# Feed-forward rows: down product one body later, two block-scale products moved from VectorE to GpSimd

## The reference, cut to what matters

```
x = x + mx_linear(silu(mx_linear(n, w_gate)) * mx_linear(n, w_up), w_down)     # n = layernorm(x)
mx_linear(a, w) = q_act(a) @ q_w(w).T
q_act(a): per block of 32 elements of a row:
    scale = 2 ** (floor(log2(max |a|)) - 2)
    q     = clip(round a / scale to 3 fraction bits, -7.5, 7.5) * scale
```

## Time and profile before

| | us |
|---|---|
| median of 3 runs | 880.72 (877.41 to 882.65) |
| the profiled execution, its own time | 882.03 |
| its span, first to last instruction | 880.0 |
| PE / DVE / POOL / ACT busy | 778.0 / 653.6 / 551.4 / 399.5 |
| mean granted PE clock | 0.957 |

### The profile page before, as it was taken

One profiled execution on the slowest core, in us unless ns is written; L12 is line 12 of the kernel. 1 busy time (PEld: TensorE's weight loads), 2 busy tenths in 40 slices (PEclk: granted clock), 3 DMA queues, 4 the chain that ended last, 5 costly groups with the idle time before them and its releaser, 6 DMA issues. The chain is left out here.

```text
span 880.0 us, 14839 instructions
## 1 busy us (share of the span) xinstructions
PE 778.0 (88%) x4808; PEld 543.6 (62%) x4808; DVE 653.6 (74%) x1162; ACT 399.5 (45%) x1074; POOL 551.4 (63%) x543
## 2 busy tenths in 40 slices
PE   3899999587999999689999999999999999756675
PEld 1545454255877777566777777777777777524443
DVE  4898998366788787656656777988697669489883
ACT  2678787442222232224554444554444444533443
POOL 3555555313666767636657778787878787445674
PEclk9899999886999999979999999999999999978999
DMA  9200000012000010042210000000000000000001
GB/s 257 87 2 0 0 0 1 1 64 95 19 19 19 18 38 33 0 144 66 69 47 1 1 1 2 1 1 1 1 1 1 1 1 1 1 0 13 18 31 37
DMA packets 8762, 24.12 MB, mean 27 GB/s; under 512 B 1711, under 2 KB 5167, under 8 KB 8087
## 3 DMA queue, kind: packets, MB, share of 16 engines
q1 hardware_dynamic: 8154, 23.28, 8.1%
q10 hardware_dynamic: 549, 0.08, 0.1%
HBM read 21.26 MB, written 2.10 MB: 27 GB/s over the span
## 5 line engine op out<-in xcount | busy, mean ns | idle before, releaser
L1457 POOL TENSOR_TENSOR q<-turned 64x512 f32<-64x512 f32 x128 | 168.2, 1314 | 28.9 <-DVE turned L1381 11.8
L1144 PE MATMUL ps<-l_yt,a 128*128 128x512 f32 x576 | 150.7, 408 | 0.3 <-DVE l_yt L1346 0.3
L1144 PEld LDWEIGHTS ps<-l_yt,a 128*128 128x128 f32 x576 | 104.8, 191 | 32.1 <-DVE turned L1381 7.3
L1278 ACT ACTIVATE p<-ps,l_negmax 128x128 f32<-128x128 f32 x256 | 91.3, 384 | 59.8 <-DVE l_negmax L1372 59.8
L1444 POOL TENSOR_TENSOR p<-p,l_inverse 128x512 f32<-128x512 f32 x64 | 67.1, 1048 | 80.1 <-DVE l_inverse L1403 79.9
L1381 DVE TENSOR_TENSOR turned<-ps,rope 128x1024 f32<-128x1024 f32 x64 | 78.0, 1219 | 37.3 <-PE ps L1144 26.3
L765 PE MATMUL ps<-yt_experts,wsplit 128*128 (+1 forms) x384 | 98.3, 406 | 4.7 <-DVE h L854 2.9
L394 DVE TENSOR_REDUCE negmax<-ps 128x4 f32<-128x512 f32 x128 | 85.3, 687 | 10.7 <-PE ps L243 8.9
L765 PEld LDWEIGHTS ps<-yt_experts,wsplit 128*128 128x128 f32 x384 | 71.3, 192 | 22.3 <-issue 4.1
L325 ACT ACTIVATE pt<-ps 128x512 f32<-128x512 f32 x128 | 72.8, 597 | 7.8 <-PE ps L263 3.8
L1393 DVE TENSOR_TENSOR turned<-ps,rope 64x512 f32<-64x512 f32 (+1 forms) x96 | 65.5, 683 | 2.4 <-PE ps L1144 1.0
(11 more groups left out here) (186 smaller groups left out, 1617.6 us busy)
## 6 DMA issues: line engine op xcount, KB each, us to landing
wide<-in_wide SPq DMA_DIRECT2D x8, 768.0 KB, 4.2
mx_raw<-in_mx SPq DMA_DIRECT2D x8, 384.0 KB, 3.1
x<-in_x SPq DMA_DIRECT2D x4, 512.0 KB, 9.3
ctx_t<-in_ctx_t SPq DMA_DIRECT2D x1, 2048.0 KB, 7.5
out<-x SPq DMA_DIRECT2D x16, 128.0 KB, 1.7
narrow<-in_narrow SPq DMA_DIRECT2D x8, 192.0 KB, 2.8
ktraw<-in_ctx_rows SPq DMA_DIRECT2D x1, 1248.0 KB
wraw<-in_gate SPq DMA_DIRECT2D x1, 1024.0 KB, 18.7
```

The source lines that it names most:

```text
L1144: out = pe.matmul(tile_ps[t % 2], a[i][:, pa, kin, k * 128:(k + 1) * 128], yt[j % 2][:, py, kin, :, :].rearrange("p b s -> p (b s)"), star ...
L1278: t = act.activation(p[:, head, s, :], s_ps[head][:, s * S:(s + 1) * S], ACT.Exp, bias=negmax[:, head, s:s + 1], accum_out=total[:, head, ...
L1457: t = pool.tensor_tensor(out[rows[(head + half) % 2], head, :], turned[rows[head], half, :], turned[rows[head], 2 + half, :], ALU.add)
```

## The change

- PE, ACT: the transposes of a batch, and their copy, move from body n-2 to n-3, the down product from n-3 to n-4, with the semaphore counts and buffer indices moved alike; `steps` has one body more (B + 7). The copy of the result stays at n-4. PE's order within a body (gate and up, down, transposes) stays.
- Last group of the front: `divide` and the product `multiply` go to POOL, ahead of its other work of bodies 5 and 7; the clip between them becomes a part of its own, `clip`, in DVE's body 5. The turn moves from PE's body 7 to 9.
- Groups 0 to 2 (latent attention): the same instructions stay on DVE in the same order; `divide` waits by itself for the scales and loses its `carry`, and the clip has one more wait.

```
-                for k, part in (..., (7, f.divide), (8, f.multiply)):
+                for k, part in (..., (7, f.divide), (8, f.clip), (8, f.multiply)):
...
-    def divide(self, dve, m, j):
-        wait(dve, self.yc_made, j)
-        carry(dve, m)
+    def divide(self, engine, m, j):
+        engine.wait_ge(self.y_step, SCALE_STEPS * (j + 1))
+        wait(engine, self.yc_made, j)
...
-    def multiply(self, dve, m, j):
+    def clip(self, dve, m, j):
         dve.wait_ge(self.y8_made, j + 1)
+        wait(dve, self.yq_made, j)
         carry(dve, m)
         dve.tensor_scalar(self.yc[:, :], self.y8[:, :], ...).then_inc(self.yc_made, 1)
-        dve.wait_ge(self.yc_made, j + 1)
-        wait(dve, self.yq_turned, j)
-        dve.tensor_tensor(self.blocks(self.yq), ...
+    def multiply(self, engine, m, j):
+        engine.wait_ge(self.yc_made, j + 1)
+        wait(engine, self.yq_turned, j)
+        engine.tensor_tensor(self.blocks(self.yq), ...
...
-        LAST, TURN_LAST = GROUPS - 1, 7
+        LAST, TURN_LAST = GROUPS - 1, 9
...
-            for n in range(B + 6):
+            for n in range(B + 7):
...                                                   # PE
-                if inside(n - 3, B):
+                if inside(n - 4, B):
-                    pe.wait_ge(hq_kept, n - 2)
-                    wait(pe, x_made, n - 4)
-                    pe.matmul(down_ps[old], m.ident[:, :], m.x[:, n - 3, :], start=True, stop=False)
+                    pe.wait_ge(hq_kept, n - 3)
+                    wait(pe, x_made, n - 5)
+                    pe.matmul(down_ps[par], m.ident[:, :], m.x[:, n - 4, :], start=True, stop=False)
...
-                if inside(n - 2, B):
-                    pe.wait_ge(hq_made, n - 1)
-                    wait(pe, hq_kept, n - 2)
+                if inside(n - 3, B):
+                    pe.wait_ge(hq_made, n - 2)
+                    wait(pe, hq_kept, n - 3)
...                                                   # ACT
-                if inside(n - 2, B):
-                    act.wait_ge(hq_turned, n - 1)
-                    wait(act, down_made, n - 3)
-                    act.activation(hqt[par][:, :], h_ps, ACT.Copy).then_inc(hq_kept, 1)
+                if inside(n - 3, B):
+                    act.wait_ge(hq_turned, n - 2)
+                    wait(act, down_made, n - 4)
+                    act.activation(hqt[old][:, :], h_ps, ACT.Copy).then_inc(hq_kept, 1)
...                                                   # DVE
-                for k, part in ((0, f.statistics), (2, f.normalise), (3, f.scales), (4, f.divide), (5, f.multiply)):
+                for k, part in ((0, f.statistics), (2, f.normalise), (3, f.scales), (5, f.clip)):
...                                                   # POOL
+                if n == 5:
+                    f.divide(pool, m, LAST)
+                if n == 7:
+                    f.multiply(pool, m, LAST)
```

More of the change, by code:

```diff
@@ L1433, in _ @@
                     normalise(n // PAIRS + 1)
-                for k, part in ((2, f.add), (3, f.statistics), (5, f.normalise), (6, f.scales), (7, f.divide), (8, f.multiply)):
+                for k, part in ((2, f.add), (3, f.statistics), (5, f.normalise), (6, f.scales), (7, f.divide), (8, f.clip), (8, f.multiply)):
                     if front_in(n, k) is not None:
@@ L1556, in scales @@
         block_scale(dve, then, self.yscale[:, :], self.yinverse[:, :], self.UNIT)
-    def divide(self, dve, m, j):
-        wait(dve, self.yc_made, j)
-        carry(dve, m)
-        dve.tensor_tensor(self.blocks(self.y8), self.blocks(self.y), spread(self.yinverse[:, :], 2, MX),
+    def divide(self, engine, m, j):
+        engine.wait_ge(self.y_step, SCALE_STEPS * (j + 1))
+        wait(engine, self.yc_made, j)
+        engine.tensor_tensor(self.blocks(self.y8), self.blocks(self.y), spread(self.yinverse[:, :], 2, MX),
                           ALU.mult, saturate=False).then_inc(self.y8_made, 1)
-    def multiply(self, dve, m, j):
+    def clip(self, dve, m, j):
         dve.wait_ge(self.y8_made, j + 1)
+        wait(dve, self.yq_made, j)
         carry(dve, m)
@@ L1568, in multiply @@
                           ALU.min, ALU.max).then_inc(self.yc_made, 1)
-        dve.wait_ge(self.yc_made, j + 1)
-        wait(dve, self.yq_turned, j)
-        dve.tensor_tensor(self.blocks(self.yq), self.blocks(self.yc), spread(self.yscale[:, :], 2, MX),
+    def multiply(self, engine, m, j):
+        engine.wait_ge(self.yc_made, j + 1)
+        wait(engine, self.yq_turned, j)
+        engine.tensor_tensor(self.blocks(self.yq), self.blocks(self.yc), spread(self.yscale[:, :], 2, MX),
                           ALU.mult).then_inc(self.yq_made, 1)
@@ L1658, in body @@
                             t.then_inc(made, 1)
-                if inside(n - 3, B):
-                    if n == 3:
+                if inside(n - 4, B):
+                    if n == 4:
                         pe.wait_ge(f.x_mid, GROUPS)
-                    pe.wait_ge(hq_kept, n - 2)
-                    wait(pe, x_made, n - 4)
-                    pe.matmul(down_ps[old], m.ident[:, :], m.x[:, n - 3, :], start=True, stop=False)
+                    pe.wait_ge(hq_kept, n - 3)
+                    wait(pe, x_made, n - 5)
+                    pe.matmul(down_ps[par], m.ident[:, :], m.x[:, n - 4, :], start=True, stop=False)
                     for k in range(FFN // 128):
-                        t = pe.matmul(down_ps[old], hqt[old][:, k * S:(k + 1) * S], m.wq[:, 2, k * E:(k + 1) * E],
+                        t = pe.matmul(down_ps[par], hqt[par][:, k * S:(k + 1) * S], m.wq[:, 2, k * E:(k + 1) * E],
                                       start=False, stop=(k == FFN // 128 - 1))
@@ L1676, in body @@
                     for k in range(FFN // 128):
-                        t = pe.transpose(h_ps[:, k * S:(k + 1) * S], hq[par][:, k * 128:(k + 1) * 128], m.ident16[:, :])
+                        t = pe.transpose(h_ps[:, k * S:(k + 1) * S], hq[old][:, k * 128:(k + 1) * 128], m.ident16[:, :])
                     t.then_inc(hq_turned, 1)
```

## The result

Eight executions each, taken side by side: 877.90 us before, 872.11 us after, by their medians. One of the eight after took 2499 us; the other seven lie between 870.11 and 875.04, their median is 870.77, and the ratio leaves the slow one out: 0.9919, 95% interval 0.9894 to 0.9945. So the change makes the kernel 0.8% faster, about 7.1 us (4.8 to 9.3). Forecast were 7.5 us less, and a time of 873.2 us (869.5 to 878.0). That time was reckoned from a median before of 880.72; from the 877.90 of this comparison, 7.5 less would be 870.4. The gain is therefore what to compare, not the time.

What follows compares the result with a forecast made beforehand. Steady feed-forward bodies alternate between DVE's own 4.64 us and 5.22, set by a round over POOL, PE and ACT. Gains of 1.82 + 1.72 + 3.12 and 0.84 in the drain, 7.5 us, gave 873.2 us (869.5 to 878.0).

Steps and rivals of the forecast that it cites:

- Divide off DVE: Feed-forward body 4: moving the last group's divide to POOL takes DVE's body from 6.46 to 4.64, gain 1.82 us.
- Clip and product: Body 5: product leaves DVE, clip stands behind one POOL product; 7.04 instead of 8.76 us, gain 1.72 (0 to 3.5).
- Shift: Transposes and down product one body later: each feed-forward body that waited falls to DVE's 4.64 us, gain 3.12.
- The round: Feed-forward loop over POOL, PE and ACT: 9.9 us carrying two bodies, 4.93 each; with three bodies, 3.3 each.
- The turn in body 9: PE's body 9: turn adds some 1.8 us before the next gate, which still ends by C(10) with 0.7 to spare.
- Drain: After the last combine: down product starts when the turned rows are there, about 0.4 us at two bodies; gain 0.84.
- PE at the lower clock: Rival: PE bodies beyond 4 and 5 at half clock lose 3.0 us each; with four, 885.2 us; chance 7%.
- Other engines within a hair: Rival: PE, ACT or POOL, within 0.8 us of DVE's pace, keep bodies near 4.9; 877.2 us; chance 14%.
- Earlier lock or full clock: Rival: clip gets the lock first (1.8 us) and the drain keeps full clock (1.7); 869.7 us; chance 12%.

Runs made afterwards that it cites:

- psum_clip: Changed kernel with the last group's clip as a scalar_tensor_tensor, lower limit read from PSUM; 66.25 us from combine 4 to last ACT copy, ratio to before 0.9867.
- shift_only: Changed kernel with the last group's divide and product back on DVE; 72.48 us from combine 4 to last ACT copy, ratio to before 0.9957.
- dve_probe: Changed kernel plus one small unused reciprocal on DVE in each body; 69.25 us from combine 4 to last ACT copy, against 68.70 for the changed kernel.
- pool_probe: Changed kernel plus one unused 128x256 product on POOL in each body; 68.73 us from combine 4 to last ACT copy, against 68.70 for the changed kernel.
- pool_only: Kernel before with the last group's divide and product on POOL, turn in PE's body 9; 76.10 us from combine 4 to last ACT copy, ratio 0.9978.

## Why the prediction was right

- *Divide off DVE:* forecast 1.82, measured 6.46 - 4.64 = 1.82; `hq` beside it back from 2.89 to 1.92.
- *Clip and product:* forecast body 5 at 7.04, measured 6.90; the clip 2.34, inside the "1.4 to 2.4", behind one POOL product. That it would be one and not none was a choice within 0 to 3.5 us of gain, and `h8` came first by only 0.13 us; but body 5 took 6.90 in all five kernels that have the divide on POOL, this clip, and nothing added to DVE or POOL. psum_clip, in which nothing stands and body 5 takes 5.77, agrees that this product is what it stood for.
- *Shift:* forecast 3.12. Over the nine bodies from C(6) to C(15) it was 44.88 before and 850.42 - 808.76 = 41.66 after, so 3.22. shift_only gives 41.62 for these nine without the other edit. dve_probe and pool_probe show DVE without idle time and POOL with slack, as reckoned. Two readings of the prediction need a correction that doesn't change its sum. The round runs over DVE as well: from combine at 841.45 to `h8` at 844.98, 3.53 of the 9.9 us are DVE's. And it wasn't the round alone: in the steady bodies of before two took 9.86, but C(6) to C(8) and C(8) to C(10) took 10.26 each. The 0.8 us more lie behind PE's long wait for `hq` in body 7, after which the granted clock was 0.50 (window 824 to 826) and the transposes took 1.04 us instead of 0.62, gate and up 2.83 instead of 1.89:

```profile
823.65 1.04 PE L1677 MATMUL ps<-ident,f_hq 128*128 128x128 bf16 x8 [2.98 <-POOL f_hq L1769]
...
824.48 2.83 PE L1656 MATMUL ps<-wq,f_yqt 128*128 128x512 bf16 x8
```

So 2.4 of the 3.22 us are the steady round, and about 0.8, by this reckoning, the lower clock in it, which the prediction had in its measured bodies without naming it.
- *The turn in body 9:* forecast hidden with 0.7 to spare; in the changed kernel PE waits 1.21 for ACT's copy there and C(10) - C(9) is 4.63. pool_only shows the price where it isn't hidden.
- *Drain:* forecast 0.84, measured 1.06. Two starts of L1667 no longer wait for the copy of an older result, only for that of the turned rows (1.48 to 1.11 of idle each, 0.7); the rest is less time at the lower clock, 1.90 for the slow L1669 but 0.73 instead of 1.09 for the L1667 pair.
- *Rivals:* from body 4 to C(15) PE at the lower clock came for one body, 6 (window 810 to 812 at 0.50), under a DVE body that hid it: it took 4.62. Other engines within a hair: no, by pool_probe. Earlier lock or full clock: not in these profiles of the changed kernel, though the full clock in the drain came in others.

So 60.10 - 53.20 = 6.90 us, and 1.06 in the drain: 7.96 us in the profile against 7.50, and 7.1 by the device times.

What I got wrong came afterwards: the two edits aren't nearly as independent as a sum of their terms looks. pool_only was worth 0.6 us in its stretch, not 2.5, as long as the round stayed critical and the turn sat in it. By device times it was worth 0.2%, with an interval that includes nothing.

## What to carry to other kernels

Follow the wait that ends last round its loop, count how many bodies the loop carries, and compare with the busiest engine's own time for one: giving the critical loop one more body of room took it off the path here, and the pace fell to that engine's own. Side jobs placed in a body are free or dear by whether the loop is critical there, so place them in a wait that exists. Where a VectorE instruction stands beside GpSimd's products, look whether its scratch data can live in PSUM, or whether another form with an input in PSUM does the same work: both times this was done here, the instruction ran at its own price.

## What the runs showed of the hardware that I had not expected

- With input and output in PSUM the exponent mask took 0.20 us instead of 1.48; in another form, with a second input in PSUM, the clip took 1.21 instead of 2.34. Both ran beside a POOL product, and with the clip POOL's next product got its 0.46 back.
- A reciprocal for whose result nobody waits cost 0.20 us of DVE's time against 0.35 in its row.
- In the drain, the same PE work with the same gaps to 0.02 us ran once at the lower clock (changed kernel, 15.50 us) and once at the full one (psum_clip, 14.22 us). What decides between them isn't visible in PE's own rows from C(15) on.
